# First expert product in two column tiles, and two slots of TensorE's expert work issued together

## What is computed

```
x = x + conv0(ln(x))   # step a, n: W_in (64 -> 168), softplus decay, state per image, norm over 128, W_out
t = t + ffn0(ln(t))    # step b: experts of layer 0
x = x + conv1(ln(x))   # step c: squares, group mix and 3x3 pooling, x * rsqrt(...)
t = t + ffn1(ln(t))    # step d: experts of layer 1

ffn(t): logits = t @ gate_w + gate_b; top 2 of 8 experts, their weights w
        for e in range(8):
            h = gelu(t @ W1[e] + b1[e])       # layer 0: 128 hidden units, layer 1: 256
            out += w[:, e:e+1] * (h @ W2[e] + b2[e])
```

## Time and profile before

| | |
|---|---|
| three runs | 725.42, 727.05, 728.75 us |
| median | 727.05 us |
| span of the profiled execution | 721.9 us |
| own time of the profiled execution | not given apart; the median is 5.15 us above its span |
| mean granted TensorE clock | 0.932 of 2.4 GHz |
| busy: TensorE, VectorE, ScalarE, GpSimd | 540.6, 523.5, 377.9, 283.2 us |
| first products, line 844 | 768 instructions, 209.9 us |
| second products, line 859 | 768 instructions, 211.3 us |
| DMA | 41.39 MB, mean 57 GB/s |

### The profile page before, as it was taken

One profiled execution on the slowest core, in us unless ns is written; L12 is line 12 of the kernel. 1 busy time (PEld: TensorE's weight loads), 2 busy tenths in 40 slices (PEclk: granted clock), 3 DMA queues, 4 the chain that ended last, 5 costly groups with the idle time before them and its releaser, 6 DMA issues.

```text
span 721.9 us, 8643 instructions
## 1 busy us (share of the span) xinstructions
PE 540.6 (75%) x3010; PEld 214.2 (30%) x3010; DVE 523.5 (73%) x926; ACT 377.9 (52%) x440; POOL 283.2 (39%) x240
## 2 busy tenths in 40 slices
PE   2314674589777988799778978798879786975776
PEld 1213223232323332343224323333333221321312
DVE  3266367868798979887998898889978796466312
ACT  2112712566566656756575657555766464543532
POOL 2122156034534453536362544365245433334013
PEclk9999975699999999999999999999999998998699
DMA  4500600063106230605041503350145005500240
GB/s 67 96 9 1 133 0 0 7 128 87 32 1 134 50 69 15 133 12 108 16 107 27 119 16 72 62 119 16 38 81 117 17 14 106 118 16 0 48 86 15
DMA packets 27834, 41.39 MB, mean 57 GB/s; under 512 B 11792, under 2 KB 19088, under 8 KB 27792
## 3 DMA queue, kind: packets, MB, share of 16 engines
q1 hardware_dynamic: 27152, 38.75, 26.2%
q0 software_dynamic: 640, 2.10, 1.0%
HBM read 38.22 MB, written 2.62 MB: 57 GB/s over the span
## 4 chain that ended last, share of the span: by engine, by line
DVE 39%; DMA 22%; PE 15%; issue 8%; POOL 7%; SPq 5%; ACT 4%; POOLq 0%; DVEq 0%; ACTq 0%
DMA WB<-w_scratch 18%; DVE nacc L1132 6%; PE yP L859 5%; PE hP L844 4%; SPq L402 3%; DMA w_scratch<-wTs 3%; DVE YW L1179 2%; POOL stat_c L486 2%; PE sA L760 2%; DVE xsplit L969 2%; PE sA L770 2%; DVE xcen_b L962 2%; POOL stat_b L486 2%; DVE xnrm L962 1%; DVE xnrm L957 1%
## 5 line engine op out<-in xcount | busy, mean ns | idle before, releaser
L691 ACT ACTIVATE H<-hP,b 128x1024 f32<-128x1024 f32 x192 | 209.2, 1110 | 82.6 <-PE hP L844 81.5
L859 PE MATMUL yP<-H,w 128*64 128x512 f32 x768 | 211.3, 632 | 21.3 <-DVE ACC L1179 19.3
L844 PE MATMUL hP<-xT,w 128*128 128x512 f16 x768 | 209.9, 399 | 4.3 <-ACT H L691 4.3
L556 POOL TENSOR_TENSOR ACC<-ACC,YW 128x512 f32<-128x512 f32 x96 | 125.6, 1313 | 194.6 <-DVE YW L1179 194.5
L844 PEld LDWEIGHTS hP<-xT,w 128*128 128x128 f16 x768 | 65.9, 101 | 145.8 <-issue 84.5
L1179 DVE SCALAR_TENSOR_TENSOR YW<-yP,b,WB 128x512 f32<-128x512 f32 x96 | 71.3, 744 | 34.2 <-PE yP L859 34.2
L859 PEld LDWEIGHTS yP<-H,w 128*64 128x64 f32 x768 | 40.1, 138 | 103.3 <-issue 89.0
L1132 DVE SCALAR_TENSOR_TENSOR nacc<-PAD,taps,nacc 128x256 f32<-128x256 f32 x112 | 60.5, 540 | 3.7
L1179 DVE SCALAR_TENSOR_TENSOR ACC<-yP,b,WB 128x512 f32<-128x512 f32 x32 | 23.1, 746 | 46.9 <-DMA WB<-w_scratch 46.9
L540 POOL TENSOR_SCALAR nrg<-nacc,go_col 128x512 f32<-128x512 f32 x8 | 12.6, 1574 | 68.9 <-ACT nacc L659 68.9
L584 ACT ACTIVATE xsq<-xcen 128x512 f32<-128x512 f32 x24 | 15.0, 626 | 36.1 <-DVE xcen L941 36.0
(11 more groups left out here) (144 smaller groups left out, 761.9 us busy)
## 6 DMA issues: line engine op xcount, KB each, us to landing
WB<-w_scratch SPq DMA_DIRECT2D x32, 1024.0 KB, 9.9
X<-in_x SPq DMA_DIRECT2D x8, 256.0 KB, 12.0
out<-X POOLq DMA_DIRECT2D x8, 256.0 KB, 2.8
H<-in_L_ffn_W SPq DMA_DIRECT2D x2, 512.0 KB, 6.2
H<-in_L_ffn_W SPq DMA_DIRECT2D x2, 256.0 KB, 4.2
w<-in_L_ffn_W SPq DMA_DIRECT2D x1, 512.0 KB, 4.8
w_scratch<-wTs SPq DMA_DIRECT2D x16, 32.0 KB, 1.8
w<-in_L_ffn_W SPq DMA_DIRECT2D x1, 256.0 KB, 4.1
```

The lines of the kernel that those rows point to most:

```text
L556: pool.tensor_tensor(ACC[l][:, cols], ACC[l][:, cols], YW[:, u % 4, :], ALU.add).then_inc(summed, 1)
L691: nc.scalar.activation(H[:, s % RING, :], hP[s % 2][:, :], ACT.Gelu, bias=b1[l][:, e * ch + c:e * ch + c + 1], scale=1.0 / WS)\
L844: mm = nc.tensor.matmul(hP[s % 2][:, hf * HALF:(hf + 1) * HALF], w1[l][:, sp, w, :], xT[l][g % 2][:, hf * HALF:(hf + 1) * HALF], start=(sp ...
L859: mm = nc.tensor.matmul(yP[hf][a * C:(a + 1) * C, :], w2[l][:, (2 * j + a) * ch + c, :], H[:, (2 * ch * j + 2 * c + a) % RING, hf * HALF:( ...
```

## The change

TensorE's first product is written as two column tiles: hidden units 0 to 63 into rows 0 to 63 of hP, units 64 to 127 into rows 64 to 127, in turn for each part of W1 and each half of the tokens, so eight matrix instructions for each chunk in place of four. `moe` of TensorE is split into `hidden` (first product) and `expert_out` (second product). In an even slot it issues both first products of the pair of slots and then both second products; in an odd slot nothing. The conditions of all waits and the order on the other engines are as before. The named steps of even slots now stand behind the products of two slots.

```diff
--- before.py
+++ after.py
@@ -827,7 +827,7 @@
                     pe.wait_ge(*c_read("send", g))
                     gate_transpose(1, g, sC)
 
-            def moe(m, s):
+            def hidden(m, s):
                 l, g = m
                 ch = CHUNKS[l]
                 if s < E * ch:
@@ -841,11 +841,16 @@
                     w = (2 * j + a) * ch + c
                     for sp in range(2):
                         for hf in range(2):
-                            mm = nc.tensor.matmul(hP[s % 2][:, hf * HALF:(hf + 1) * HALF], w1[l][:, sp, w, :],
-                                                  xT[l][g % 2][:, hf * HALF:(hf + 1) * HALF],
-                                                  start=(sp == 0), stop=(sp == 1))
+                            for b in range(2):
+                                mm = nc.tensor.matmul(hP[s % 2][b * C:(b + 1) * C, hf * HALF:(hf + 1) * HALF],
+                                                      w1[l][:, sp, w, b * C:(b + 1) * C],
+                                                      xT[l][g % 2][:, hf * HALF:(hf + 1) * HALF],
+                                                      start=(sp == 0), stop=(sp == 1))
                     mm.then_inc(h_ready, 1)
 
+            def expert_out(m, s):
+                l, g = m
+                ch = CHUNKS[l]
                 unit = y_unit(m, s)
                 if unit:
                     j, hf, c = unit
@@ -861,6 +866,14 @@
                                               start=(c == 0), stop=(c == ch - 1))
                     if c == ch - 1:
                         mm.then_inc(y_ready, 1)
+
+            def moe(m, s):
+
+                if s % 2 == 0:
+                    hidden(m, s)
+                    hidden(m, s + 1)
+                    expert_out(m, s)
+                    expert_out(m, s + 1)
 
             def final(m, half):
```

## The result

The changed kernel takes 742.01 us (median of 4 runs, 740.82 to 743.65), the kernel before 726.23 beside it (723.67 to 728.75). The ratio is 1.0226, with a 95% interval of 1.0198 to 1.0254: slower, as forecast, by 16 us where 26 had been worked out. The span of the profiled execution went from 721.9 to 739.8 us, and the changed kernel's profiled execution took 741.61 us by its own time.

The account below looks back on a forecast made before the run. A loop through VectorE and two transfers was taken to bound the kernel. Terms 17.0 + 8.4 + 1.9 + 1.1 + 0.3 - 2.7 gave +26 us: span 748, plus 5.15 kept to the median, 753 us; range 740 to 766.

Parts of the forecast that it names:

- What bounds: Steady-state period: a loop through VectorE and two transfers, 75.4 us for four images; TensorE has 11 us free.
- Tiles and switches: First products: tiles run side by side, keeping 0.87 us; fewer switches save TensorE 3.0 us a group, off the loop.
- The rival of tiles in turn: First products' halves run one after the other, 1.73 us each; kernel at 800 to 850 us; chance 5%.
- Gate of layer 1, +1.5: Slot 6: gate behind two first and two second products, so top-2 starts 1.5 us later in groups 1 to 5.
- my sign of 2.6: Slot 6: VectorE's wait before the scale ahead of layer 1's top-2 would be near 2.6 us.
- Final transpose, +1.9: Slot 8: transpose queued behind second product 9, which waits for VectorE; final add waits 1.9 us in groups 1 to 5.
- Transpose of c, +1.4: Slot 18: products 19 go ahead (0.1), plus gelu delays through ScalarE's order from slots 10 to 13 (2.2); middle 1.4 us.
- Group 0 was put at +0.3: First group: gate +1.5 us, offset by half-clock products 9 now ahead of y1; 0.3 us in all.
- The tail was put at -2.7: Behind the last spread: seven second and six first products without gaps, 1.6 us of half clock kept; 2.7 us less.
- "Faster": Rival: TensorE's saved 3.0 us a group reach the end of the loop, giving 700 to 706 us; chance 8%.
- "No change": Rival: moved waits come to half; room ahead of the spread's landing and the tail absorb the rest, 724 to 731; 6%.
- "Second product 9 alone": Rival: only slot 8 costs, the gate stays near where it was; about 737 us; chance 10%.

Follow-up runs that it names:

- e1: The kernel before with the column tiles alone, order untouched: 723.95 us, ratio 0.9972.
- e2: The changed kernel with first products in the whole array again, so only the pairing of slots stays: 752.55 us, ratio 1.0355.
- e3: The changed kernel with layer 1's first final transpose one slot earlier in TensorE's order, ahead of second product 9: 729.86 us, ratio 1.0082.
- e5: The changed kernel with the odd second product back in its own slot in slots 12 to 18 alone: 732.87 us, ratio 1.0111.
- e6: The changed kernel with the odd second product back in its own slot in slot 18 alone: 736.95 us, ratio 1.0175.
- e10: The changed kernel with slots 6 to 9 in the order before, one first and one second product in each slot: 728.22 us, ratio 1.0043.
- e11: e4 with slots 6 and 7 in the order before: 720.36 us, ratio 0.9939.
- e7: The changed kernel with the odd second product back in its own slot in slot 6 alone: 748.21 us, ratio 1.0312.
- e8: e4 with layer 1's first final transpose also moved to slot 7: 721.96 us, ratio 0.9956.
- e9: e4 without the column tiles, first products in the whole array again: 719.97 us, ratio 0.9926.
- e4: The changed kernel with first products still in pairs but each second product issued in its own slot: 719.10 us, ratio 0.9910.

## Why the prediction was right, and where its sum was off

**What bounds.** Right. e1 saves 16.9 us of TensorE's busy time (523.7 against 540.6), and its five periods take 75.9 us in the mean, as before.

**Tiles and switches.** Right in both: 0.875 us for a first product and no gap to the second. With the whole array the switch to the second product costs 0.08 in e2's row (forecast 0.10 to 0.15). The rival of tiles in turn is out. The Trainium skill says that a change of tiling mode drains TensorE (TensorEngine Tiling (Array Packing), Key Properties), and e2's row agrees, with 0.08 us for this switch; what it is worth is set by the loop.

**Gate of layer 1, +1.5.** Too much, and the term of the sum that failed. VectorE's top-2 stands 0.7 later behind the scale of layer 0's landing (S). I had put down 0.7 for a longer wait for output 6 and the rest for the gate behind it. The first did not come in the mean (1.94 us, 1.92 before): my sign of 2.6 was reached in group 5 alone. The second came as 0.58 and was paid back by 0.67 in the subtraction, which ends with GpSimd's addition; I hadn't followed what VectorE does right behind the gate. e3 gives the price of the late gate without the wait for the transpose: S and T together are 13.75 against 13.32 before, some 0.4 in a period and not 1.5. The half clock spreads it: S grew by 1.0 in group 3 and by 2.4 in group 5, where the pair of first products took 3.19 and 3.03 us, and was 0.3 and 0.4 shorter in groups 1 and 4 (1.92 and 2.17 us).

**Final transpose, +1.9.** Right: 1.85 to 2.74 in five groups. By e3 its removal takes 1.65 from T, and 12 us from the kernel. T grew by 1.0 only, from 8.27 to 9.26, since the subtraction took 0.67 less and a multiplication of the gate weights (L1019, after L1032), which had run beside GpSimd's addition before (0.73 us), 0.5 less.

**Transpose of c, +1.4.** Q and the stretch behind it rose by 1.75 (1.95 less 0.2); both parts of the reasoning hold (e5, e6). The value was a middle between 0.1 and 2.2 and came out a little low.

**Not foreseen.** In groups 3 and 4 layer 0's weights take longer to come: R is 16.9 and 17.4 there, and its growth makes 3.2 of the 18 us. The sum has no term for it. It made up for a part of what the gate didn't cost, so by luck the total came out nearer to the sum than its terms did. SyncE's rows in the changed kernel, write and read-back of the weights, in group 3:

```profile
372.18 0.48 SPq L436 DMA_DIRECT2D w_scratch<-wTs  x1
375.34 1.23 SPq L442 DMA_DIRECT2D WB<-w_scratch  x2
```

The write took 3.1 us; before, 1.8 (367.13 to 368.93). The DMA view of these 3.2 us (372.2 to 375.4) shows what else was under way, one packet of 16 KB on queue q8, which the profile names the instruction queue:

```profile
q8 instruction: 1, 0.02, 2.0%
...
w_scratch<-wTs SPq DMA_DIRECT2D x1, 32.0 KB, 3.1
```

The 13 traces hold 208 such writes. In 25 of them the read-back was issued 2.4 to 3.7 us after the write, and in each of the 25 a packet of q8 began 0.3 to 1.6 us after the write's issue. The other 183 took 1.80 to 1.88, and only one of these had a packet of q8 in that time. So a write that meets such a packet is the long one. Why it costs that much isn't shown, and no run moved a packet on purpose. The kernels with tiles have 768 more matrix instructions and move 30 or 31 packets on q8, the three without 24 or 25; all kernels with tiles meet one in group 3 (R 16.2 to 18.2), none of the three without does (15.5).

**The two ends.** Group 0 was put at +0.3 and came out at -2.3. While VectorE waits for the first landing, TensorE now has both first products behind it, and after the landing only second products and y0 follow. Timelines of TensorE, before:

```profile
89.93 1.15 PE L859 MATMUL yP<-H,w 128*64 128x512 f32 x4 [4.14 <-DVE ACC L1179]
91.00 2.07 PE L770 MATMUL sA<-KVs,ctS 16*128 16x128 f32 x8
93.01 1.89 PE L844 MATMUL hP<-xT,w 128*128 128x512 f16 x4
94.82 3.31 PE L859 MATMUL yP<-H,w 128*64 128x512 f32 x8
98.07 1.15 PE L770 MATMUL sA<-KVs,ctS 16*128 16x128 f32 x8
```

and after:

```profile
90.26 1.94 PE L864 MATMUL yP<-H,w 128*64 128x512 f32 x8 [1.53 <-DVE ACC L1192]
92.13 1.15 PE L770 MATMUL sA<-KVs,ctS 16*128 16x128 f32 x8
93.22 1.08 PE L864 MATMUL yP<-H,w 128*64 128x512 f32 x4
94.89 1.08 PE L864 MATMUL yP<-H,w 128*64 128x512 f32 x4 [0.59 <-DVE YW L1192]
95.90 1.15 PE L770 MATMUL sA<-KVs,ctS 16*128 16x128 f32 x8
```

The engine stood idle for less long (1.53 us, 4.14 before) and ran at full clock, where from 92 to 94 us it had been granted 0.50 before; y1 begins 2.2 us sooner. I had seen the half clock here, but not that it would go. The traces of the variants go the same way: the kernel before, e1, e10 and e11, which have no second first product ahead of the landing, idled 2.5 to 5.1 us and ran on at half clock for a part, and end group 0 at 165.9 to 167.8 us (its weights of layer 1). The changed kernel and e2 to e6 idled 1.3 to 1.9 and kept full clock, and end it at 162.3 to 164.3. e7, e8 and e9 idled 1.5 to 1.7 and fell below full clock all the same, at 163.7 to 166.6, so the shorter idle time doesn't settle it by itself. The tail was put at -2.7. From the scale behind the last landing to the end it is 24.1 us rather than 28.3, 4.2 less. Another 0.8 is luck: the last write of the weights took 1.8 us, and in the kernel before 2.6, beside a packet on q8. Chain of waits of the changed kernel, in which pairs follow each other at 1.73 and 1.72:

```profile
716.64 1.94 PE yP L864 x8
718.58 1.73 PE hP L845 x16
720.31 1.72 PE yP L864 x8
...
727.20 5.16 PE yP L864 x24
```

Here the surcharge of half clock that I kept (1.6) is nearly gone: the first pair took 1.94. Together: the periods 3.6 below the sum, group 0 2.6, tail 2.7, against 0.7 more in group 7. That is the whole distance from 26 to 18 us of span. The median I had put at 753, 11 us above the measured 742; 8 of them are this distance, and 3 come from the 5.15 us that I kept between span and median, which is 2.2 in the changed kernel.

**Signs.** 1536 instructions, the pace of 0.87, no gap, and the wait of 1.9 in five groups came as written. The scales behind the landings of layer 1's spread stand 77.3 to 80.9 us apart (forecast 79 to 81 for the landings). The wait of 2.6 for output 6 and a top-2 later by 1.5 did not come.

**Rivals.** "Faster" fell with e1: the 3.0 us in a group never reached VectorE. "No change" fell too: the room ahead of the landing took none of the longer Q and T. "Second product 9 alone" is not it either: e3 removes it and 5 us of loss remain.

## What to carry to other kernels

Batching like products on an in-order engine moves every step between them behind the whole batch. Look at each such step for a ring: product waits for consumer, step stands behind product, and consumer waits for step. Batch only what has no one else waiting behind it (here the first products); that (e4) was 0.9% faster than the kernel before, where the full batch was 2.3% slower.

## What was not expected of the hardware

A VectorE subtraction of 64 elements in each partition took 1.00 us when it began 0.34 us after a GpSimd addition and 0.33 when it began 1.01 us after it. Both times it ended 0.08 us behind the addition, so that a later start cost nothing. A 32 KB write that takes 1.8 us took 2.4 to 3.7 wherever a packet of the instruction queue began 0.3 to 1.6 us behind it, but for one case. And an idle time of 2.4 us was followed by full clock in group 1 and by half clock in group 3: sixteen instructions took 1.92 us and 3.19.
